# The second attention's PE order: the products with v between the two heads' tiles of a slot

## The reference, cut to what matters

```python
qkv = x @ qkv_w.T + qkv_b              # 8 samples, 256 tokens, 16 heads of 8
q = q * cos + _rotate_half(q) * sin    # and k alike
attn = jnp.einsum('abhqd,abhkd->abhqk', q, k) * scale
attn = jax.nn.softmax(attn, axis=-1)
out = jnp.einsum('abhqk,bhkd->abhqd', attn, v)
out = out @ proj_w.T + proj_b
```

## Time and profile before

| | |
|---|---|
| median of 3 runs | 1129.2 us (1124.94 to 1131.93) |
| the profiled execution | 1133.85 us, span 1132.1 us, mean granted clock 0.855 |
| the stage, from the first exponential to the end of the last copy | 693.1 to 796.4 us |
| instructions of the program | 17427 |

### The profile page before, as it was taken

How to read it: one execution, slowest core, us unless ns; L and a number is a source line. 1 busy time by engine, 2 the same in 40 slices (tenths; PEclk the granted TensorE clock), 3 DMA queues, 4 the chain that set the end, 5 groups by cost and what they waited for, 6 DMA issues and landing times. The chain is left out here.

```text
span 1132.1 us, 17427 instructions
## 1 busy us (share of the span) xinstructions
PE 983.3 (87%) x5403; PEld 712.0 (63%) x5403; DVE 979.8 (87%) x1490; ACT 698.0 (62%) x799; POOL 355.5 (31%) x214
## 2 busy tenths in 40 slices
PE   6756776677759999999999899999759999999997
PEld 5533444343437888888888555544547888888886
DVE  7799888888977999999999787996697999999996
ACT  4689999999964445555544553677434455554443
POOL 2035655566440333434331120100012343433330
PEclk9865555555558999999999998999969999999999
DMA  2000000000105755555550000000037655555521
GB/s 56 1 1 1 1 1 1 1 1 1 36 14 139 201 152 153 149 154 146 154 149 18 1 1 1 2 1 1 8 88 189 164 150 152 146 152 150 158 81 37
DMA packets 36478, 85.16 MB, mean 75 GB/s; under 512 B 5968, under 2 KB 19280, under 8 KB 36432
## 3 DMA queue, kind: packets, MB, share of 16 engines
q1 hardware_dynamic: 36432, 84.56, 28.0%
HBM read 82.45 MB, written 2.10 MB: 75 GB/s over the span
## 5 line engine op out<-in xcount | busy, mean ns | idle before, releaser
L1335 ACT ACTIVATE sg<-ps 128x512 f32<-128x512 f32 x264 | 156.7, 593 | 266.3 <-PE ps L473 264.8
L473 PE MATMUL ps<-xh,whi 128*128 128x512 f32 x528 | 206.5, 391 | 1.3 <-ACT b L1200 1.3
L473 PE MATMUL ps<-xh,wlo 128*128 128x512 f32 x528 | 205.9, 390 | 0.0
L473 PE MATMUL ps<-xl,whi 128*128 128x512 f32 x528 | 205.7, 390 | 0.0
L2081 DVE TENSOR_TENSOR hf<-sg,ps 128x512 f32<-128x512 f32 x264 | 170.4, 684 | 35.4 <-DVE hl L2088 24.6
L1482 POOL TENSOR_TENSOR rr<-xr,rr 128x2048 f32<-128x2048 f32 x32 | 144.9, 4551 | 159.4 <-ACT xr L1179 94.9
L1529 POOL CAST whi<-wraw 128x384 fp32r<-128x384 f32 x66 | 67.1, 1017 | 372.5 <-PE ps L473 288.4
L2088 DVE TENSOR_TENSOR hl<-hf,hh 128x1024 fp32r<-128x1024 f32 x132 | 179.2, 1358 | 0.5 <-DVE hf L2081 0.5
L2093 DVE TENSOR_TENSOR hf<-hf,cbc 128x1024 f32<-128x1024 f32 x128 | 157.7, 1232 | 13.4
L1383 ACT ACTIVATE hh<-hf 128x1024 fp32r<-128x1024 f32 x132 | 139.2, 1055 | 5.0 <-DVE hf L2093 5.0
L1531 POOL TENSOR_TENSOR wlo<-wraw,whi 128x384 fp32r<-128x384 f32 x66 | 117.4, 1779 | 5.3
(11 more groups left out here) (262 smaller groups left out, 1594.6 us busy)
## 6 DMA issues: line engine op xcount, KB each, us to landing
cbc<-routing_coefficients SPq DMA_DIRECT2D x256, 256.0 KB, 3.8
wraw<-in_wexp_dram SPq DMA_DIRECT2D x66, 192.0 KB, 2.7
X<-in_x_dram SPq DMA_DIRECT2D x4, 256.0 KB, 4.4
routing_coefficients<-cT SPq DMA_DIRECT2D x8, 128.0 KB, 2.3
out_dram<-X SPq DMA_DIRECT2D x4, 256.0 KB, 2.9
rope_in<-in_consts_dram SPq DMA_DIRECT2D x1, 512.0 KB, 3.3
wa<-in_wA_dram SPq DMA_DIRECT2D x1, 256.0 KB, 3.8
w_in<-in_wB_dram SPq DMA_DIRECT2D x1, 128.0 KB, 3.2
```

The costliest lines, as they stand in the source:

```text
L473: return pe.matmul(o, l, r, start=start, stop=stop, **kw)
L1335: act.activation(sg[c % 2][:, :], bank(4 + 2 * (c % 2)), ACT.Silu).then_inc(s_sg, 1)
```

## The change

In a slot, `pv_b` is called by `b_tiles` between the tile of head 0 and that of head 1, ahead of head 1's wait for `s_mx`. Its own waits (for the exponentials, and every fourth slot for the copy of bank 6) and its four matmuls are what they were. Nothing else moves; no instruction is added or removed.

```diff
-            def b_tiles(U, V):
+            def b_tiles(U, V, between=None):
...
                 for i in range(2):
+                    if i == 1 and between is not None:
+                        pv_b(between // 2, between % 2)
                     if scores and V >= 1:
                         pe.wait_ge(s_mx, 2 * (V - 1) + i + 1)
...
                 for U in range(B * UNITS + 3):
                     V = U + AHEAD
-                    b_tiles(U, V)
-                    if U >= 3:
-                        pv_b((U - 3) // 2, (U - 3) % 2)
+                    b_tiles(U, V, U - 3 if U >= 3 else None)
                     if V < (B + 1) * UNITS:
                         b_max_step(V)
```

## The result

The changed kernel takes 1190.4 us (median of 6 runs, 1186.4 to 1192.9) against 1128.3 us for the kernel before (median of 6 runs). The ratio is 1.0545 with a 95% interval of 1.052 to 1.057: slower by 5.5%, 62 us. The forecast was slower by 19.9 us, 1149.1, and the range ended at 1158.

A forecast was written before the change was run, and what follows sets the result against it. The stage was taken as a chain of hand-overs with PE and DVE near full, the DVE within 6% of being the bound. Terms 18.6 + 3.0 - 1.4 - 0.3 = +19.9 us on 1129.2 gave 1149.1 us, range 1140 to 1158.

The forecast's parts named there:

- The wait for the copy: Slots 4n+7: products wait for ACT's copy of bank 6, exponentials across it 2.79 us apart, 15 times; +18.6 us.
- The filled slots: Slots 2 to 10, with two filling matmuls in front: tiles no longer overlap, 15.56 us against 12.58; +3.0 us.
- The steady slots: Ordinary slots: the DVE's idle moves from the first maximum to the second; 0.2 us a sample gained, -1.4 us.
- The wait for the exponentials: Products in slot U need exponential U-2 at the latest, already waited for at the slot's top; costs nothing.
- The sum: Whole stage: 18.6 + 3.0 - 1.4 - 0.3 = +19.9 us, added to the median 1129.2 for 1149.1 us.
- the PE's clock falls in the stalls: Rival: half clock for half of the stage, about 19 us a sample there, 14 more, 1163 us; chance 0.09.
- the loss is half swallowed: Rival: DVE and PE catch up behind each stall, 14.8 us a sample, 12 us lost, 1141 us; chance 0.10.
- The other side: Rival: products fill t1's wait for its maximum, gaining 4.9 us, 1124 us; chance 0.04 together with no effect.
- The drain on a change of tiling mode: Counter-rule: row-tile to column-tile changes drain the PE, 0.07 us each, some 30 more; adds 2 us, 1151.

The follow-up runs named there:

- e3_waiting_only: The kernel before, with the products between the tiles only in the slots that wait for the copy of bank 6; 1151.5 us, ratio 1.023.
- e5_fill_fit: The changed kernel, with unneeded matmuls filling the PE's idle time ahead of the products in slots that wait for the copy; 1153.8 us, ratio 1.022.
- e9_fill_late: The changed kernel, with 3 or 4 unneeded matmuls ahead of the waiting products only from slot 31 on; 1166.7 us, ratio 1.030.
- e8_copy_first_middle: The kernel before, with products between the tiles in slots 12 to 52 only, and those slots' copies ahead of the exponential on ACT; 1131.9 us, ratio 1.0025.
- e4_copy_first: The changed kernel, with each copy of bank 6 ahead of the same slot's exponential on ACT instead of behind it; 1137.6 us, ratio 1.0069.
- e7_before_no_fill: The kernel before, without its own two filling matmuls in each of slots 0 to 11; 1138.7 us, ratio 1.0123.
- e2_waiting_behind: The changed kernel, with the products behind the tiles again only in the slots that wait for the copy; 1182.0 us, ratio 1.045.

## Why the prediction was wrong, point by point

**The direction was right, and so was the total at the full clock.** *The wait for the copy:* 2.79 us was forecast, and 2.79 or 2.80 was measured at the full clock in the changed kernel's two stalls, in nine of ten of e3_waiting_only and in e5_fill_fit up to slot 34. The PE's idle time in it was forecast at 0.9 or 1.3; e9_fill_late had 0.85 and 1.09. *The filled slots:* forecast +3.0, 15.56 us for seven intervals. The changed kernel has 8.55 (exponential 2 at 690.31 to 6 at 698.86) and 6.51 (7 at 701.65 to 10 at 708.16), together 15.06, so +2.5. *The steady slots:* the sample at the full clock took 15.41 us where the prediction had 15.4, and the second maximum does wait in place of the first: without any stall at the copy a sample takes 13.37. *The wait for the exponentials* cost nothing: no matmul of the changed kernel waited for one from 680 to 850 us. *The sum:* 1149.1 forecast, 1147.0 and 1149.3 in the two runs of e5_fill_fit with the kernel before's mean clock.

**That sum held by luck in part, as two of its terms were off by about as much in opposite directions.** The prediction said that nothing buys the stalls' 2 x 1.26 = 2.52 us a sample back, and that the ordinary slots win 0.2. e3_waiting_only has the stalls without the ordinary slots' split, 14.43 us a sample; e8_copy_first_middle has the split without the stalls, 13.38; both together take 15.41, and neither 13.16. So the stalls cost 1.27 by themselves and 2.03 on top of the split, less than 2.52 either way. And the split costs 0.22 by itself and 0.98 on top of the stalls, where a gain was forecast. Together that is 2.25, and 2.3 had been added up.

**The step that failed is the clock.** The forecast took 1.00 for the whole stage. I had the fall as a rival, "the PE's clock falls in the stalls", at 0.09 and 1163 us. Three things in it were wrong.

- Its chance. I weighed the stalled stretch, 2.1 busy of 3.41, against a stretch of the tail with 2.72 of 3.42 that had kept 1.00, and took that for cover. The changed kernel's clock fell at the end of a stretch with 2.60 of 3.40. The row I set against the rival had hardly more than that.
- Its length. I took the clock to be down for half of the stage. Once down it stayed down, from 712.5 to 862.6. A slower PE does not end the stalls, because ACT's 1.02 and 0.59 us don't depend on the PE's clock. The PE's idle time in the two stalls was 0.85 and 1.09 at the full clock (e9_fill_late) and 0.28 and 1.71 at half: about 2 us a sample at both. Had I asked whether the state would end by itself, the order of before would have said so: there the slow PE has no gap left.
- Its price. I had 19 us for a sample at half clock. It is 21.3, since the terms of the chain that are the PE's grow too: 3.53 across the copy, twice a sample. Over the 137.6 us at half clock, 6.45 samples of 21.3, that is 5.9 x 6.45 = 38 us above the full-clock sample of 15.4. With the 19.9 of the forecast that makes 58 of the stage's 60.0 us. The 4.9 more behind the stage and the 5.9 less ahead of it nearly cancel; the medians are 62 us apart.

**The other rivals.** That the loss is half swallowed had 14.8 us a sample, and 15.41 came; where the stalls stood alone (e3_waiting_only) it did happen, at 14.43. The other side, that the products would fill the wait for the maximum, needed the copy to be out of the way. e4_copy_first and e8_copy_first_middle put it out of the way, and still gained nothing: neither won any of the 0.76 us of DVE idle, as the second maximum's wait takes its place. The drain on a change of tiling mode (the Trainium skill, "TensorEngine Tiling (Array Packing)", "Key Properties") would have given 1151. Two microseconds can't be told from 1147.0 and 1149.3, but the starts can tell: in a filled slot of the changed kernel t0, products and t1 start at 706.59, 707.02 and 707.59, which is 0.43 and 0.57 apart, the distances of the earlier trace rows. No drain shows beside the lost overlap.

**What stays open.** What makes the clock fall in one stall and not in the next isn't settled. e3_waiting_only passed ten stalls; the traced execution of the changed kernel fell behind its second, and that of e9_fill_late, the same code up to there, behind its fourth. The busy share doesn't foretell it, as a stretch of e3_waiting_only and one of e4_copy_first show, the second of them just before its clock fell:

```profile
750.00:753.41 3.41, 1.95 (x31) 0.95 (x28) 2.25 (x5) 1.87 (x4) 0.00 (x0) 1.00 0.00 0
```

```profile
780.39:783.80 3.41, 3.41 (x28) 1.92 (x20) 0.99 (x2) 2.24 (x3) 0.00 (x0) 1.00 0.00 0
```

With 1.95 us of 3.41 busy the clock stayed; behind a stretch shown as wholly busy it fell. How much of the tail's fall in e4_copy_first is the split of the tiles there wasn't tried by itself. Nor is it settled how long the PE must go without a gap before the clock comes back: it took 17 us in e5_fill_fit, 25.5 in e9_fill_late and 44 in e7_before_no_fill. In e2_waiting_behind, where the PE's largest gap in the steady part was 0.77 us, once in a sample of 20.08, it didn't come back in over 100 us.

## What to carry to other kernels

Before an instruction with a wait is moved forward in an engine's program, follow back what releases the wait: here the products waited for a copy that stood behind an exponential that needed the very tile now queued behind the products, and the chain of 2.79 us could be read off the profile. Then ask of any new stall on the PE whether it is periodic and released by an engine that the PE's clock doesn't touch. If so, price the half clock for the whole stage too, not for a part only: here only filled gaps ended it within the stage. A sum that comes out is no proof of its terms; the two parts of this change had to be run apart to see that each was off. Matmuls that nobody needs, put into the gap, are a cheap test (35 us here), but taking the wait away is the better repair (53 us).

## What the runs showed of the hardware that I had not expected

The PE's clock has two lasting states in one and the same code. In the order of before, half clock ended by itself after 44 us, with the PE busy 43.80 of 43.80 us. With gaps of 1.71 and 0.28 us in a sample of 21.32 it lasted 150 us. With the gaps filled it ended 25.5 us after the last one (749.5 to 775.0). And 69 added matmuls in a stage made a kernel faster by 35 us.
